# A mixing layer whose token sums are taken with the cosine and sine of twice the angle, and whose layer-norm scale, shift and bias move to ACT and PE

## What is computed

```python
x1, x2 = (t_rot[..., 0::2], t_rot[..., 1::2])          # first 128 of 256 columns
rot_half = jnp.stack([-x2, x1], axis=-1).reshape(t_rot.shape)
# _rotary(t) = concatenate([t_rot * cos + rot_half * sin, t_pass])
Xn = _layernorm(X, gamma, beta)
QKV = Xn @ W_in + b_in
Q, K, V = jnp.split(QKV, 3, axis=-1)
K = _rotary(K, ROT_DIM)
V = _rotary(V, ROT_DIM)
A = jnp.sum(_cos_sim(K) * _cos_sim(V), axis=-2)         # one vector of 256, summed over the tokens
A = (1.0 - IDENTITY_WEIGHT) * A + IDENTITY_WEIGHT
Y = A[:, None, :] * Q
Y = Y @ W_out + b_out
return Y + X
```

## Time and profile before

| | |
|---|---|
| median of 3 runs | 1245.53 us (1245.0 to 1249.11) |
| the profiled execution | 1249.32 us |
| its span, first to last instruction | 1247.6 us |
| busy over the span | PE 982.1 us (79%), DVE 671.2 (54%), PE weight loads 567.3 (45%), ACT 493.1 (40%), POOL 306.9 (25%) |
| mean granted TensorE clock | 0.895 of full |
| mixing phase | from 802.87 us (SP's first load) to 924.12 us (POOL's last power), of the span |
| first key/value matmul, last product, first y matmul | 841.39, 885.84, 901.67 us |

### The profile page before, as it was taken

One profiled execution on the slowest core, in us unless ns is written; L12 is line 12 of the kernel. 1 busy time (PEld: TensorE's weight loads), 2 busy tenths in 40 slices (PEclk: granted clock), 3 DMA queues, 4 the chain that ended last, 5 costly groups with the idle time before them and its releaser, 6 DMA issues. The chain is left out here.

```text
span 1247.6 us, 23402 instructions
## 1 busy us (share of the span) xinstructions
PE 982.1 (79%) x9002; PEld 567.3 (45%) x9003; DVE 671.2 (54%) x1764; ACT 493.1 (40%) x792; POOL 306.9 (25%) x367
## 2 busy tenths in 40 slices
PE   4632899999999999896069999518567599999994
PEld 1420244444445445263047767413345556666662
DVE  3843999999999999155300000198775612122121
ACT  1320066767767767844022222063126422222220
POOL 2003011021021021132412222135820034444441
PEclk9775599999999999997569999859778899999998
DMA  5299700000000000006414555300036622232233
GB/s 190 44 145 132 105 3 2 3 3 2 3 2 3 3 3 3 2 1 198 178 39 111 160 127 144 80 0 1 1 90 231 220 43 44 45 46 46 42 46 84
DMA packets 79690, 81.88 MB, mean 66 GB/s; under 512 B 22800, under 2 KB 71568, under 8 KB 79344
## 3 DMA queue, kind: packets, MB, share of 16 engines
q1 hardware_dynamic: 65200, 61.44, 19.4%
q0 software_dynamic: 12288, 17.10, 8.3%
q10 hardware_dynamic: 2112, 2.10, 0.5%
HBM read 58.45 MB, written 24.13 MB: 66 GB/s over the span
## 5 line engine op out<-in xcount | busy, mean ns | idle before, releaser
L566 ACT ACTIVATE prob<-p_s 128x1024 f32<-128x1024 f32 (+3 forms) x320 | 269.0, 894 | 109.8 <-PE p_s L509 109.6
L497 PE MATMUL p_p<-k_ks,k_qs 112*32 112x512 bf16 (+3 forms) x2560 | 227.3, 374 | 58.7 <-PEq L270 38.9
L591 DVE TENSOR_REDUCE mpart<-p_p 128x1 f32<-128x512 f32 x384 | 248.9, 684 | 8.7 <-PE p_p L497 7.0
L509 PE MATMUL p_s<-k_qs,k_ks 114*32 114x512 bf16 (+3 forms) x2560 | 177.3, 349 | 5.7 <-ACT prob L566 2.9
L497 PEld LDWEIGHTS p_p<-k_ks,k_qs 112*32 112x32 bf16 x2560 | 76.1, 95 | 177.2 <-DVE mpart L591 67.2
L524 PE MATMUL p_o<-prob,k_vaug 128*32 128x512 f32 (+3 forms) x1280 | 147.6, 529 | 2.5 <-DVE k_oT L608 1.9
L684 POOL TENSOR_SCALAR_AFFINE_SELECT prob<-prob 128x256 f32<-128x256 f32 x128 | 51.7, 408 | 361.0 <-ACT prob L566 359.6
L588 DVE CUSTOM_DVE_ANT_0 unread<-p_p,causal 128x128 bf16<-128x128 f32 (+3 forms) x256 | 120.5, 484 | 6.9 <-PE p_p L497 4.6
L509 PEld LDWEIGHTS p_s<-k_qs,k_ks 114*32 114x32 bf16 x2560 | 73.5, 97 | 83.8 <-issue 27.4
L1869 DVE TENSOR_TENSOR mid<-silu_g,e_u 128x512 f32<-128x512 f32 x39 | 26.8, 687 | 138.7 <-PE e_u L1763 138.7
L1358 DVE SCALAR_TENSOR_TENSOR outr<-p_o,rows,k_mod 128x256 f32<-128x256 f32 x16 | 7.7, 484 | 141.5 <-PE p_o L1315 141.5
(11 more groups left out here) (284 smaller groups left out, 1267.8 us busy)
## 6 DMA issues: line engine op xcount, KB each, us to landing
r_raw<-in_L_ffn_w_dram SPq DMA_DIRECT2D x24, 512.0 KB, 6.0
k_wi<-in_L_ffn_wi_dram SPq DMA_DIRECT2D x8, 1024.0 KB, 5.1
k_wo_e<-in_L_ffn_wo_dram SPq DMA_DIRECT2D x8, 1024.0 KB, 7.3
k_qs<-q_dram SPq DMA_DIRECT2D x28, 256.0 KB, 9.4
sum<-k_x SPq DMA_DIRECT2D x8, 512.0 KB, 6.8
wmod<-in_L_wmod_dram SPq DMA_DIRECT2D x2, 1536.0 KB, 12.2
q_dram<-q_parts SPq DMA_DIRECT2D x12, 256.0 KB, 13.1
disp<-zeros SPq DMA_DIRECT2D x2, 1310.0 KB, 19.3
```

The lines of the kernel that those rows point to most:

```text
L497: last = nc.tensor.matmul(p1[n % 3][32 * j:32 * (j + 1), 0:w], k.qs[0:KROWS, qt // TQ, GH * G + hs, q0:q0 + 32], k.ks[0:KROWS, QC * ck:QC ...
L509: last = nc.tensor.matmul(sc[pair][32 * j:32 * (j + 1), i, off:QC], k.ks[0:KALL, k0:k0 + 32], k.qs[0:KALL, c, GH * g + 2 * pair + i, off:Q ...
L566: nc.scalar.activation(prob[:, u % 2, 2 * pair:2 * pair + 2, off:QC], sc[pair][:, :, off:QC], ACT.Exp, scale=HD ** -0.5).then_inc(e_done, 1)
L591: nc.vector.reduce_max(mpart[:, hs, qt, ck:ck + 1], p1[n % 3][:, 0:w], AX.X).then_inc(p1_used, 1)
```

## The change

In the mixing phase:

- Keys and values are no longer rotated. For a pair of columns, the rotated product is a sum and a difference: the even and odd products of rotated columns are half of (K0 V0 + K1 V1) plus or minus half of a term in the cosine and sine of twice the angle. Four sets of 128 columns are therefore summed over tokens per tile: the plain products (2 sets), the plain products of the first 128 columns times the cosine, and the crossed products (even times odd) times the sine. The table `rot_t` holds these factors, computed for twice the angle.
- DVE per tile: copy the values out of PSUM (`vals`), multiply by the keys straight from PSUM (256 columns), multiply crossed (128 columns). POOL per tile: one operation over 256 columns with the table. Both norms are of unrotated keys and values.
- The bias of keys and values enters on PE: one bf16 matmul of `share` (1/64 and 1/32) with `b_part`, the bias in three bf16 parts on three groups of partitions, ahead of each output's two float32 matmuls. Keys and values are separate outputs of 256 columns with two buffers each.
- gamma and beta are per partition of the transposed copy, so ACT applies them while it copies `xnT` out of PSUM. DVE's two operations per quarter go.
- All engines' lists are written in another order: first products stand between the last layer-norm steps; ACT's squares between its normalizations; the token sums of quarters 0 and 1 between the tiles of quarters 2 and 3. `w_tok` is made by POOL. The gate on `w_out` and `b_out` and `bq_rep` move behind tile 7. After the last sum DVE needs eight small operations instead of one copy. ACT scales one half of `w_out`.
- The loads of gamma and beta (128 KB each, replicated) become small ones, behind the others, in router 0.

The core of the diff:

```diff
@@ load_mix
-    load(k.gamma[:, :], a.L1_attn_gamma.partition_broadcast(P))
-    load(k.beta[:, :], a.L1_attn_beta.partition_broadcast(P))
...
+    for dst, src in ((k.gamma, a.L1_attn_gamma), (k.beta, a.L1_attn_beta), (k.bq, a.L1_attn_b_in[0:D])):
+        sp.dma_start(dst[:, :], src.rearrange("(t p) -> p t", p=P),
+                     allow_slow_non_contiguous=True).then_inc(k.mix_in, 16)
@@ phase_mix, gpsimd
+            nc.gpsimd.memset(w_tok[:, :, :], 0.0).then_inc(tok_zero, 1)
+            def turn_products(i):
+                pool.wait_ge(prod_ready, i + 1)
+                nc.gpsimd.tensor_tensor(prods[:, i, 2:4, :], prods[:, i, 0::3, :], rot_t[:, i, :, :],
+                                        ALU.mult).then_inc(trig_ready, 1)
+            def token_weights(q):
                 pool.wait_ge(norm_ready, 2 * TQ * (q + 1))
...
+                pool.wait_ge(inv_ready, q + 1)
+                nc.gpsimd.tensor_tensor(w_tok[:, s, 0], inv_n[:, s, 0], inv_n[:, s, 1], ALU.mult).then_inc(w_ready, 1)
@@ phase_mix, vector
+            def products(i):
+                keys, values = pk[i % 2][:, :], vals[:, i % 2, :]
+                dve.wait_ge(v_done, i + 1)
+                if i >= 2:
+                    dve.wait_ge(norm_ready, 2 * (i - 1))
+                nc.vector.tensor_copy(values, pv[i % 2][:, :]).then_inc(vals_ready, 1)
+                dve.wait_ge(vals_ready, i + 1)
+                dve.wait_ge(norm_ready, 2 * i + 1)
+                tt(prods[:, i, 0:2, :].rearrange("p s d -> p (s d)"), keys, values, ALU.mult)
...
+                tt(prods[:, i, 3, :].rearrange("p (n two) -> p n two", two=2), kp, vp[:, :, ::-1],
+                   ALU.mult).then_inc(prod_ready, 1)
+            step(nc.vector.tensor_copy(b_part[:, :], b_kv[:, :]))
...
-            nc.vector.tensor_copy(A_rows[:, :], pA[:, :]).then_inc(Arow_ready, 1)
+            nc.vector.tensor_scalar(A_rows[:, R2:D], pA[:, R2:D], 2.0, None, ALU.mult)
+            nc.vector.tensor_copy(A_mix[:, :], pA[:, D:D + R2])
+            step(nc.vector.tensor_copy(A_sum[:, :], plain[:, :, 0]))
+            tt(A_sum[:, :], A_sum[:, :], plain[:, :, 1], ALU.add)
+            step(tt(A_mix[:, :], A_mix[:, :], pA[:, D + R2:2 * D], ALU.add))
+            step(tt(A_dif[:, :], mixed[:, :, 0], mixed[:, :, 1], ALU.add))
+            tt(out[:, :, 0], A_sum[:, :], A_dif[:, :], ALU.add)
+            tt(out[:, :, 1], A_sum[:, :], A_dif[:, :], ALU.subtract).then_inc(Arow_ready, 1)
@@ phase_mix, scalar
+            def turned(q):
+                for half in range(KH):
+                    act.wait_ge(tp_done, 2 * q + half + 1)
+                    nc.scalar.activation(xnT[:, half, QC * q:QC * (q + 1)], tp[half][:, :], ACT.Identity,
+                                         bias=k.beta[:, half:half + 1], scale=k.gamma[:, half:half + 1]).then_inc(xnT_ready, 1)
...
+            outer(0)
+            outer(1)
+            outer(2)
+            nested(0)
+            turned(0)
+            outer(3)
+            nested(1)
             for q in range(NC):
+                squares(TQ * q)
+                squares(TQ * q + 1)
+                if q + 1 < NC:
+                    turned(q + 1)
+                squares(TQ * q + 2)
+                if q + 2 < NC:
+                    nested(q + 2)
+                squares(TQ * q + 3)
@@ phase_mix, tensor
+            def keys_values(i):
+                pe.wait_ge(xnT_ready, 2 * (i // TQ) + 2)
+                for out, n, used, done in ((pv, 2, vals_ready, v_done), (pk, 1, prod_ready, k_done)):
+                    if i >= 2:
+                        pe.wait_ge(used, i - 1)
+                    nc.tensor.matmul(out[i % 2][:, :], share[:, :], b_part[:, D * (n - 1):D * n], start=True, stop=False)
+                    for t in range(KH):
+                        last = nc.tensor.matmul(out[i % 2][:, :], xnT[:, t, P * i:P * (i + 1)], w_in[:, t, D * n:D * (n + 1)],
+                                                start=False, stop=(t == KH - 1))
+                    last.then_inc(done, 1)
...
+                keys_values(TQ * q)
+                keys_values(TQ * q + 1)
+                if q + 1 < NC:
+                    turn(q + 1)
+                keys_values(TQ * q + 2)
+                if q >= 2:
+                    sum_products(q - 2)
+                keys_values(TQ * q + 3)
+            sum_products(NC - 2)
+            sum_products(NC - 1).then_inc(A_done, 1)
@@ consts
+    twice = 2.0 * angle.astype(np.float64)
     rot = np.zeros((T, 2, ROT, 2), np.float32)
+    rot[:, 0, :, 0] = np.cos(twice)
+    rot[:, 0, :, 1] = -np.cos(twice)
+    rot[:, 1, :, :] = -np.sin(twice)[:, :, None]
```

More of the change, by code:

```diff
@@ L1417, in phase_mix @@
         w_c = sb("w_c", [P, KH, D])
-        b_kv = k.b_kv
-        b_out = k.b_out
-        bq = k.bq
         bq_rep = sb("bq_rep", [P, KH, P])
[L1422 to L1427, removed]
+        b_part, b_rest = sb("b_part", [P, 2 * D], BF), sb("b_rest", [P, 2 * D])
+        share = sb("share", [P, P], BF)
+        vals = sb("vals", [P, 2, D])
         sq = sb("sq", [P, 4, D])
@@ new lines, in _ @@
+            gate = k.mod[:, 1, GA, :]
+            stats(0)
+            stats(1)
+            outer_bias(0)
+            stats(2)
+            outer_bias(1)
+            modulate(0)
+            outer_bias(2)
+            nested_stats(0)
+            stats(3)
+            nested_bias(0)
+            modulate(1)
+            outer_bias(3)
+            nested_stats(1)
+            modulate(2)
+            nested_bias(1)
+            products(0)
+            nested_stats(2)
+            products(1)
@@ new lines, in _ @@
+            modulate(3)
+            nested_bias(2)
+            products(2)
+            nested_stats(3)
+            products(3)
+            nested_bias(3)
+            for i in range(TQ, NT):
+                products(i)
+                if i == 2 * TQ - 1:
+                    tt(w_out[:, :, :], w_out[:, :, :], bcast(gate, KH), ALU.mult).then_inc(wout_ready, 1)
+                    tt(b_out[:, :], b_out[:, :], gate, ALU.mult).then_inc(wout_ready, 1)
+                    nc.vector.tensor_copy(bq_rep[:, :, :], last_bcast(bq[:, :], P)).then_inc(wout_ready, 1)
@@ L1583, in _ @@
+            step(tt(A_dif[:, :], mixed[:, :, 0], mixed[:, :, 1], ALU.add))
+            out = A_rows[:, 0:R2].rearrange("p (n two) -> p n two", two=2)
+            tt(out[:, :, 0], A_sum[:, :], A_dif[:, :], ALU.add)
+            tt(out[:, :, 1], A_sum[:, :], A_dif[:, :], ALU.subtract).then_inc(Arow_ready, 1)
             dve.wait_ge(A_done, 2)
-            step(nc.vector.tensor_scalar(A[:, :], pAt[:, :], 0.5, 0.5, ALU.mult, ALU.add))
-            for t in range(KH):
-                last = nc.vector.tensor_scalar(w_sc[:, t, :], w_out[:, t, :], A[:, t:t + 1], None, ALU.mult)
@@ L1626, in squares @@
                                          accum_out=norm2[:, i, s:s + 1]).then_inc(norm_ready, 1)
[L1628 to L1636 removed]
+            act.wait_ge(weights_in, 16 * MIX_LOADS)
@@ L2034, in build @@
         k.bq = sbuf(mixer, "bq", [P, KH])
[L2035 to L2036 removed]
+        k.gamma = sbuf(mixer, "gamma", [P, KH])
+        k.beta = sbuf(mixer, "beta", [P, KH])
         k.rot_t = sbuf(mixer, "rot_t", [P, NT, 2, 2 * ROT])
```

282 lines of the change are left out of this document (118 added, 164 removed).

## The result

The changed kernel took 1227.29 us (median of 4 runs, 1226.65 to 1227.63), the kernel before 1246.51 beside it: ratio 0.9843, 95% interval 0.9824 to 0.9862. The profiled execution took 1227.63 us, its span 1225.9. The forecast was 1232.2 in 1224 to 1243: right in direction and range, 4.9 us too slow.

What follows compares the result with a forecast made beforehand. DVE was taken to bound the layer norms and tile loop, latency and waits the chain. -19.1 + 0.8 + 4.5 + 0.5 = -13.3 us from the median of 1245.53 gave 1232.2, range 1224 to 1243.

Steps and rivals of the forecast that it cites:

- Part 1, first matmul: Layer norms up to the first key/value matmul: it comes at 824.4 in place of 841.39, 17.0 us earlier.
- the preparation of the bias: Before x lands: six operations that split the bias take about 3.5 us and cost 0 to 1, taken as 0.
- Part 2, last product: Loop over 16 tiles: PE sets the pace at 1.93 to 2.08 us; last product at 867.0, before 886.1: -19.1.
- no charge for PSUM-fed products: DVE's products with keys from PSUM do not wait for POOL; if they did, 0 to 2 us worse.
- Part 3, the weights: From last product to token weights: POOL's last tile, power and small product take 3.1 us, before 2.3: +0.8.
- The chain: From token weights to first y matmul: small DVE operations wait for POOL's; 17.8 us, before 13.25: +4.5.
- The y loop: Its start waits for POOL's last operation, ending 3.1 us after y's start, before 2.6: +0.5.
- Rival 1: In the chain, L1608 and L1609 slip in before POOL's next turn, saving 2.4 us each: 1226.5; chance 0.15.
- Rival 2: In the tile loop, handoffs between PE, ACT and DVE set the pace, not PE: 1235.2 to 1244.8; chance 0.20.
- rival 3: In the tile loop, PE's clock stays at 0.50: last product 31.0 us later than forecast, 1263; chance 0.10.
- rival 4: First matmul is not earlier because ACT's list holds it, though keys and values paths gain; no chance of its own.
- the phases outside don't move: Sign: phases before 803 and after router 1's start keep their length, else the reading of the blocks is wrong.

Runs made afterwards that it cites:

- the second profile of the kernel before: The kernel before, run and profiled once more with nothing changed: 1247.74 us, ratio 1.0007.
- the bias runs: The changed kernel with each bf16 bias matmul of keys and values issued twice, or with none: 1232.11 us (0.9888) and 1229.39 us (0.9862).
- the two placings inside the loop: The changed kernel with two quarters of POOL's gate operations in the product loop, two behind scaled `w_out`, or all four in the loop: ratios 0.9870 and 0.9864.

## Why the prediction was right, and where it was off

- **Part 1, first matmul** (-17.0): measured -16.6. The list written with old durations held within 0.4 us; the preparation of the bias did lie in the shade of x's loads. Most of it is the new order of the lists: with gamma and beta back on DVE the first matmul still comes 14.0 earlier than before, while their move in the old order brings 0.4.
- **Part 2, last product** (-19.1): measured -20.1, and -19.3 against the second profile of the kernel before, so the closeness is good to about 0.8. PE sets the pace, at 1.95 a tile, the low end of 1.93 to 2.08; no charge for PSUM-fed products was right. POOL's operation took 0.72, not 0.9.
- **Part 3, the weights** (+0.8): measured +0.4, from that 0.72 and from 0.20 for the small product (0.35).
- **The chain** (+4.5): measured +1.7; this is the mis-sized step. The forecast had two whole waits, at L1608 and L1609, and parts of one at L1606 (1.3 to 2.4) and L1614. L1606 was ready at 869.4 just as POOL's operation ended, and started in the gap, 0.23 in place of ending at +5.0 from the weights: it ended at +2.6, and all behind it moved up by that. The sum of 512 columns at full clock, 1.06, put it there; the forecast had it 2.6 to 3.7 us behind the weights, and it was 2.4. The kind of step was right, as the run with POOL held back shows: 4.9 us of waits were left in the chain.
- **The y loop** (+0.5): measured +0.1.
- The sum for the phase was -13.3 and is -17.9: 1.0 from the last product, 0.4 from the weights, 2.8 from the chain, 0.4 from the loop. Of medians the gain is 1246.51 - 1227.29 = 19.2; no stage of the phase accounts for the other 1.3, and it is no more than the spread of the parts outside.
- **Rival 1** (1226.5) gave nearly the time, but not by its mechanism: L1608 and L1609 waited in full (L1609 escaped in one experiment only). What escaped was the operation ahead of them, and that its time came out is luck. By the rule of the Trainium skill ("SBUF — State Buffer", section "Who interferes with whom") whoever issues first holds the shared ports for its whole instruction; the page writes it of DVE's two-port modes, and L1608 and L1609 contend by its line on operations with two SBUF inputs. The trace agrees for operations as short as these, which took 2.25 and 2.37, and L1606 started in a gap. **Rival 2** falls by the bias runs, **rival 3** by the clock of 1.00 from 830 on, **rival 4** by the first matmul. That the phases outside don't move held to 1.6 and 2.2 us, where the two profiles of the kernel before differ by 1.5 and 0.7. That all of the 2.2 is spread is likely and not shown.

## What to carry to other kernels

Work taken off the busiest engine of a stage gains only when the in-order lists of the others can use it: gamma and beta moved alone gained nothing, with the lists rewritten they were worth up to 13.5 us. DVE's small SBUF-only operations each cost up to a whole POOL operation when POOL works beside them. Moving POOL's work elsewhere pays only where DVE has no such operations: held back until `w_out` was scaled it gave 4.0 of the 5.8 us back, and in the two placings inside the loop the phase ended 1.2 and 2.5 us later than in the changed kernel. Where a chain of such operations meets a row of POOL's, its time depends on tenths of a microsecond in when it starts. One wait more or fewer is one POOL operation, 2.4 us, so such a term wants a range of that size.

## Not expected of the hardware

- A 64-column DVE operation can start in the 0.07 us in which POOL waits between two dependent operations of 2.4 us (L1606, 0.23; L1609, 0.21 without the bias). POOL's next operation then took 2.41 and 2.35, at most 0.1 more than usual, while the DVE operations beside it took 1.55 to 2.37. The pattern 0.23, 2.25, 2.37 stood in six profiled executions, 1.55, 2.26, 0.21 in one: it seems to hang on when the chain meets POOL's row. That the gap is what lets it in is read from the rows and wasn't tested alone.
- A plain float32 copy within SBUF waits for POOL like an operation with two inputs (`m_bq_rep`: 0.29 alone, 2.42 beside POOL), and so does the bias L125 of 4 columns (0.15 and 2.30).
- After the last product the clock stayed at 1.00 over 3 us in which PE worked 0.14.
